# A macaron block (MoE, state-space scan, MoE) on one core: four-column-group tiles with block transposition, a second token buffer and a longer scan

## The reference

```python
def ffn(x):
    scores = sigmoid(x @ w_router.T)
    topk_w, topk_i = top_k(scores, 2)
    topk_w = topk_w / sum(topk_w)
    h = silu(einsum('th,eih->tei', x, wg)) * einsum('th,eih->tei', x, wu)
    out = einsum('te,teh->th', comb, einsum('tei,ehi->teh', h, wd))
    return out + shared_experts(x)

def attn(x):
    p = einsum('bld,ed->ble', x, W_xproj)
    dt, B, C = softplus(p[..., :256]), p[..., 256:272], p[..., 272:]
    h = exp(dt * A) * h + dt * B * x
    y = einsum('bdn,bn->bd', h, C) + D * x

x = x + 0.5 * ffn(layernorm(x))
x = x + attn(layernorm(x))
x = x + 0.5 * ffn(layernorm(x))
```

## Time and profile before

| | |
|---|---|
| time, median of three runs (all three) | 521.38 us (520.27, 521.38, 522.26) |
| span of the profiled execution, first to last instruction | 517.8 us |
| around the span, against the median | 3.6 us |
| PE busy, share of the span | 506.7 us, 98% |
| PE weight loads | 423.2 us, 82% |
| DVE, POOL, ACT busy | 324.0, 231.4, 158.6 us |
| DMA, over the span | 67.91 MB, 131 GB/s |

### The profile page before, as it was taken

The page is one execution under the profiler, slowest core; times in us unless marked ns, Lnnn a source line. Parts: engine busy times, 40 slices in busy tenths (PEclk is TensorE's granted clock), DMA queues, the critical chain, the costliest instruction groups (busy, mean ns, idle before and its releaser), DMA issues.

```text
span 517.8 us, 11713 instructions
## 1 busy us (share of the span) xinstructions
PE 506.7 (98%) x4666; PEld 423.2 (82%) x4667; DVE 324.0 (63%) x658; ACT 158.6 (31%) x337; POOL 231.4 (45%) x208
## 2 busy tenths in 40 slices
PE   8998999999999999999989999999999899999997
PEld 6998996568979999557979799975598899955696
DVE  3844338123747999997679399999967532422225
ACT  1111122221156434553203643445521111122210
POOL 1051000602216999995454289999920650000032
PEclk9999999999999999999999999999999999999999
DMA  7958999512415455541322445545200231210012
GB/s 231 392 231 303 394 389 346 178 59 66 129 36 142 118 139 135 163 117 30 113 63 71 129 94 121 156 131 155 73 22 2 72 101 52 82 42 14 20 54 81
DMA packets 42232, 67.91 MB, mean 131 GB/s; under 512 B 5152, under 2 KB 24992, under 8 KB 42176
## 3 DMA queue, kind: packets, MB, share of 16 engines
q1 hardware_dynamic: 29424, 38.94, 26.5%
q10 hardware_dynamic: 9088, 18.09, 9.4%
q0 software_dynamic: 3664, 10.10, 6.1%
HBM read 48.89 MB, written 18.22 MB: 130 GB/s over the span
## 4 chain that ended last, share of the span: by engine, by line
PE 90%; DVE 6%; DMA 2%; issue 1%; ACT 0%; POOL 0%; DVEq 0%; POOLq 0%; ACTq 0%
PE ps L526 40%; PE ps L551 20%; PE ps L541 14%; PE ps L564 7%; PE ps L570 2%; PE ps L575 2%; PE ps L707 2%; DMA bcb<-bc_rows 1%; PE ps L718 1%; PE ps L748 1%; DVE hb L1054 1%; DMA bc_rows<-hh 1%; DVE hb L1058 0%; PE ps L609 0%; PE ps L759 0%
## 5 line engine op out<-in xcount | busy, mean ns | idle before, releaser
L526 PEld LDWEIGHTS ps<-xt,w_gu 128*128 128x128 f32 x1400 | 161.6, 192 | 5.7 <-issue 3.8
L526 PE MATMUL ps<-xt,w_gu 128*128 128x128 f32 x1400 | 163.8, 276 | 0.4 <-DVE xres L1069 0.4
L1054 DVE SCALAR_TENSOR_TENSOR hb<-hb,ps 128x640 f32<-128x640 f32 x68 | 55.4, 815 | 121.3 <-ACT hb L800 121.2
L551 PE MATMUL ps<-w_dn,hb 128*128 128x256 f32 x520 | 120.8, 380 | 0.0
L551 PEld LDWEIGHTS ps<-w_dn,hb 128*128 128x128 f32 x520 | 94.8, 190 | 10.8
L800 ACT ACTIVATE hb<-ps 128x640 f32<-128x640 f32 x68 | 47.6, 700 | 176.9 <-PE ps L526 163.0
L526 PE MATMUL ps<-xnt,w_gu 128*128 128x128 f32 x680 | 80.5, 276 | 3.0 <-DVE xres L1069 2.7
L1099 DVE TENSOR_TENSOR_SCAN ps<-ps,region 128x512 f32<-128x512 f32 x64 | 78.3, 1223 | 8.1 <-POOL region L1018 6.2
L1032 POOL TENSOR_TENSOR xnt<-xnt,hh 128x512 f32<-128x512 f32 x64 | 82.2, 1286 | 2.5 <-DVE hh L1104 2.5
L526 PEld LDWEIGHTS ps<-xnt,w_gu 128*128 128x128 f32 x680 | 78.7, 192 | 5.5 <-DVE xres L1069 3.1
L998 POOL DMA_INDIRECT region<-yg_rows,ypos x32 | 30.5, 954 | 110.2 <-DMA yg_rows<-ob 88.4
(11 more groups left out here) (112 smaller groups left out, 302.0 us busy)
## 6 DMA issues: line engine op xcount, KB each, us to landing
bcb<-bc_rows SPq DMA_DIRECT2D x22, 512.0 KB, 5.1
region<-bc_rows SPq DMA_DIRECT2D x10, 512.0 KB, 5.0
w_gu<-in_wg ACTq DMA_DIRECT2D x7, 640.0 KB, 9.8
xg<-xg_rows SPq DMA_DIRECT2D x35, 128.0 KB, 4.2
w_gu<-in_wu ACTq DMA_DIRECT2D x7, 640.0 KB, 11.2
w_dn<-in_wd ACTq DMA_DIRECT2D x7, 640.0 KB, 13.8
yg_rows<-ob SPq DMA_DIRECT2D x20, 128.0 KB, 3.5
xg_rows<-bcb SPq DMA_DIRECT2D x1, 2176.0 KB, 14.9
```

The lines of the kernel that those rows point to most:

```text
L526: last = nc.tensor.matmul(gup(p)[:, c * P:(c + 1) * P], w_gu4[:, e, k, c * P:(c + 1) * P], x, start=(k == 0), stop=(k == KC - 1))
L551: ins = nc.tensor.matmul(outp(p), hb[:, p, c * P:(c + 1) * P], w_dn4[:, e, c, :], start=(c == 0), stop=(c == IC - 1))
L1054: nc.vector.scalar_tensor_tensor(out=h, in0=h, scalar=1.0, in1=gup(p)[:, 0:I], op0=ALU.add, op1=ALU.mult).then_inc(s_a, 1)
```

## The change

What it does, part by part:

- Of the four mixed tiles of a segment one stays, `(7, 6, 6)` with the one free group left. The other groups go into three quad tiles of four fixed groups of 32 rows (`QUADS`).
- A quad tile's gate-up takes one group of 32 rows at a time, as the stationary operand of all four column groups; column group q multiplies with the inner columns q x 32 to q x 32 + 31 of each 128 (`quad_piece`), 320 or 160 moving columns in runs of 32. The hidden rows lie in PSUM by quarters; after the products, of which the second is split in two, DVE transposes the 128 x 640 result in blocks of 32 x 32 (`nc.vector.transpose`), and the down-projection `down_quad` reads it as it is.
- `xnt` gets a second buffer, one per half; all shared tiles read it, and the copies to DRAM with their loads, transposes and ACT copies go. The row addresses move by 512 (one `pos` in place of `pos` and `ypos`).
- Gathered rows and the buffers of the overflow loop get the tile `gathered`, and two waits for the result of the scan (`s_yadd`) go. The scratch for POOL's transfer descriptors is set to 4,096 bytes.
- In segment 1 the routed tiles come after two shared ones in place of five. Both scans are dealt out over 13 tiles, and the steps around their ends are set anew.

```diff
-MIXED = [(5, 5, 5), (0, 0, 2), (1, 1, 3), (6, 6, 7)]
+MIXED = [(7, 6, 6)]
+QUADS = [(5, 5, 5, 3), (0, 0, 0, 2), (2, 1, 1, 1)]
...
+QUAD = I // 4
...
-ROUTED = [("whole", e, e) for e in range(WHOLE)] + [("mixed", None, m) for m in range(MT)]
+ROUTED = [("whole", e, e) for e in range(WHOLE)] + [("quad", None, m) for m in range(len(QUADS))] + [("mixed", None, m) for m in range(MT)]
 ORDERS = [SHARED[0] + SHARED[1][:1] + ROUTED + SHARED[1][1:],
-          SHARED[0] + SHARED[1][:1] + ROUTED + SHARED[1][1:],
+          SHARED[0][:2] + ROUTED + SHARED[0][2:] + SHARED[1],
...
-SHARES = [[2, 2, 3, 2, 3, 3, 2, 3, 3, 3, 3, 3], [2, 2, 3, 2, 3, 3, 2, 3, 3, 3, 3, 3]]
+SHARES = [[2, 3, 2, 3, 3, 2, 2, 2, 3, 2, 3, 2, 3], [2, 2, 2, 3, 3, 3, 2, 3, 2, 2, 2, 3, 3]]
...
-    ("X1", 0), ("scan", S1 + 1, S1 + 13, 0), ("first", S1 + 13), ("Y", 0), ("N1", "P", 2), ("N2", "P", 2), ("second", S1 + 13),
-    ("O", 1), ("G", 1), ("first", S1 + 14), ("T", "P", 2), ("second", S1 + 14), ("R1", 2),
-    ("scored and ranked", S1 + 15, 2), ("S", 2, 0), ("second", S1 + 15), ("tiles", S2 - 1, S2),
-    ("C", 1, 0, TT), ("N1", "A", 1), ("S", 2, 1), ("tiles", S2, S2 + 1), ("N2", "A", 1), ("table", 2),
-    ("first", S2 + 1), ("T", "A", 1), ("second", S2 + 1), ("X1", 1),
-    ("scan", S2 + 2, S2 + 14, 1), ("first", S2 + 14), ("Y", 1), ("N1", "P", 3), ("N2", "P", 3), ("second", S2 + 14),
-    ("first", S2 + 15), ("T", "P", 3), ("second", S2 + 15), ("O", 2), ("R1", 3),
+    ("X1", 0), ("scan", S1 + 1, S1 + 14, 0), ("first", S1 + 14), ("Y", 0), ("N1", "P", 2), ("N2", "P", 2),
+    ("second", S1 + 14), ("O", 1), ("G", 1), ("first", S1 + 15), ("T", "P", 2), ("second", S1 + 15), ("R1", 2),
+    ("scored and ranked", S2 - 1, 2), ("second", S2 - 1), ("C", 1, 0, TT), ("N1", "A", 1), ("S", 2, 0), ("N2", "A", 1),
+    ("tiles", S2, S2 + 1), ("table", 2), ("first", S2 + 1), ("T", "A", 1), ("second", S2 + 1), ("X1", 1), ("S", 2, 1),
+    ("scan", S2 + 2, S2 + 15, 1), ("first", S2 + 15), ("Y", 1), ("N1", "P", 3), ("N2", "P", 3), ("second", S2 + 15),
+    ("T", "P", 3), ("O", 2), ("R1", 3), ("scored and ranked", S2 + 16, 3), ("S", 3, 0), ("S", 3, 1), ("second", S2 + 16),
...
-        gat = region[:, 2048:4096].rearrange("p (t s h) -> p t s h", t=TT, s=2)
+        gathered = sb("gathered", [P, TT * 2 * H])
+        gat = gathered[:, :].rearrange("p (t s h) -> p t s h", t=TT, s=2)
...
-        xnt = sb("xnt", [P, KC, HALF])
+        xnt = sb("xnt", [P, 2, KC, HALF])
...
-                        x = xt[:, p, k, :] if loaded(n) else xnt[:, k, t * P:(t + 1) * P]
+                        x = xt[:, p, k, :] if routed(n) else xnt[:, segment(n) % 2, k, t * P:(t + 1) * P]
...
+            def quad_piece(n, j, g0, g1):
+                p, e = n % 2, QUADS[index_of(n)][j]
+                gate = p * 1536 + j // 2 * 512 + j % 2 * QUAD
+                up = p * 1536 + (1024 + j // 2 * QUAD if j % 2 else j // 2 * 512 + 2 * QUAD)
+                for k in range(KC):
+                    w = w_gu4[:, e, k, :].rearrange("p (g c q i) -> p g c q i", g=2, c=IC, q=4)
+                    for q in range(4):
+                        r = q * GROUP
+                        if g1 - g0 == 2:
+                            dst = ps[r:r + GROUP, gate:gate + 4 * QUAD].rearrange("p (g w) -> p g w", g=2)[:, :, 0:QUAD]
+                        else:
+                            a = up if g0 else gate
+                            dst = ps[r:r + GROUP, a:a + QUAD]
+                        last = nc.tensor.matmul(dst, xt[:, p, k, j * GROUP:(j + 1) * GROUP], w[:, g0:g1, :, q, :],
+                                                start=(k == 0), stop=(k == KC - 1))
+                return last
+
+            def gate_up_quad(n, c0):
+                if c0 == 0:
+                    return quad_piece(n, 0, 0, 2)
+                if c0 == 2:
+                    return quad_piece(n, 1, 0, 1)
+                if c0 == 4:
+                    quad_piece(n, 2, 0, 2)
+                    return quad_piece(n, 3, 0, 1)
+                quad_piece(n, 1, 1, 2)
+                return quad_piece(n, 3, 1, 2)
...
+            def down_quad(n):
+                p = n % 2
+                for c in range(IC):
+                    for j in range(4):
+                        r, a = j * GROUP, j * QUAD + c * GROUP
+                        ins = nc.tensor.matmul(outp(p)[r:r + GROUP, :], hb[:, p, a:a + GROUP],
+                                               w_dn4[:, QUADS[index_of(n)][j], c, :],
+                                               start=(c == 0), stop=(c == IC - 1))
+                return ins
...
             def rows_of(n):
-                if n + 2 < TILES and loaded(n + 2):
+                if n + 2 < TILES and routed(n + 2):
...
-                        pool.dma_start(xg_dram[s % 2][0:HALF, :].rearrange("(t p) h -> p t h", p=P),
-                                       xn["P"]).then_inc(s_rows[s], 16)
...
-                nc.vector.tensor_tensor(h, h, gup(p)[:, I:GU], ALU.mult).then_inc(s_h, 1)
+                if kind_of(n) == "quad":
+                    p = n % 2
+                    even, odd = h[:, :, 0:QUAD], h[:, :, QUAD:2 * QUAD]
+                    nc.vector.tensor_tensor(even, even, quad_banks(p)[:, :, 2 * QUAD:3 * QUAD], ALU.mult).then_inc(s_hq, 1)
+                    dve.wait_ge(s_up, n + 1)
+                    nc.vector.tensor_tensor(odd, odd, ps[:, p * 1536 + 1024:p * 1536 + 1024 + 2 * QUAD]
+                                            .rearrange("p (a w) -> p a w", a=2), ALU.mult).then_inc(s_hq, 1)
+                    dve.wait_ge(s_hq, 2 * quads_upto(n))
+                    nc.vector.transpose(hb[:, p, :], hb[:, p, :]).then_inc(s_h, 1)
...
-    nc = bacc.Bacc("TRN2", target_bir_lowering=False, num_devices=1)
+    nc = bacc.Bacc("TRN2", target_bir_lowering=False, num_devices=1, dynamic_dma_scratch_size=4096)
```

More of the change, by code:

```diff
@@ L23 @@
 GROUP = 32
-MIXED = [(5, 5, 5), (0, 0, 2), (1, 1, 3), (6, 6, 7)]
+MIXED = [(7, 6, 6)]
+QUADS = [(5, 5, 5, 3), (0, 0, 0, 2), (2, 1, 1, 1)]
 MT = len(MIXED)
 STATIC0 = WHOLE * P
-FREE0 = STATIC0 + MT * 3 * GROUP
-OWN = [g for tile in MIXED for g in tile]
+QUADS0 = STATIC0 + MT * 3 * GROUP
+FREE0 = QUADS0 + len(QUADS) * P
+OWN = [g for tile in MIXED + QUADS for g in tile]
 ROOM = [(P if e < WHOLE else 0) + GROUP * OWN.count(e) for e in range(E)]
@@ L85, in last_routed, with quads_upto, moves @@
 def last_routed(s):
-    return s * SEG_TILES + max(j for j, t in enumerate(ORDERS[s]) if t[0] == "mixed")
-def loaded(n):
-    return n % SEG_TILES not in DIRECT[segment(n)]
+    return s * SEG_TILES + max(j for j, t in enumerate(ORDERS[s]) if t[0] != "shared")
 def turned(n):
[L95 to L100, removed]
+    return sum(1 for m in range(n + 1) if routed(m))
+def quads_upto(n):
+    return sum(1 for m in range(n + 1) if kind_of(m) == "quad")
 def mixed_upto(n):
     return sum(1 for m in range(n + 1) if kind_of(m) == "mixed")
-def moves(n, q, which):
-    return sum(2 if kind_of(m) == "mixed" else 1 for m in range(n + 1) if m % 2 == q and which(m))
+def moves(n, q):
+    return sum(2 if kind_of(m) == "mixed" else 1 for m in range(n + 1) if m % 2 == q and routed(m))
 def half_states(first, n, part):
@@ L293, in build @@
         s_ones = sem("s_ones")
-        s_rows = [sem(f"s_rows{s}") for s in range(SEGS)]
         s_alog = sem("s_alog")
@@ L402, in load_rows @@
                 else:
-                    a = m * P if kind_of(n) == "shared" else (TT + m) * P
+                    a = QUADS0 + m * P if kind_of(n) == "quad" else m * P
                     sp.dma_start(xg[:, q, :], rows[a:a + P, :]).then_inc(s_xg[q], 16)
@@ L415, in store_rows @@
                 else:
-                    sp.dma_start(rows[m * P:(m + 1) * P, :], ob[:, q, :]).then_inc(s_y[q], 16)
+                    a = QUADS0 + m * P if kind_of(n) == "quad" else m * P
+                    sp.dma_start(rows[a:a + P, :], ob[:, q, :]).then_inc(s_y[q], 16)
             def fetch_rows(m):
-                if m >= TILES or not loaded(m):
+                if m >= TILES or not routed(m):
                     return
                 s = segment(m)
-                if m == first_shared_load(s):
-                    sp.wait_ge(s_rows[s], 16)
                 if m == first_routed(s):
@@ L588, in first_use @@
                             weights_in(e, k)
+                elif kind_of(n) == "quad":
+                    for e in dict.fromkeys(QUADS[index_of(n)]):
+                        weights_in(e, k)
                 elif kind_of(n) == "whole" or index_of(n) == 0:
@@ L659, in second @@
                     rows_of(n)
-                    down_fixed(n).then_inc(s_dn, 1)
+                    down = down_quad if kind_of(n) == "quad" else down_fixed
+                    down(n).then_inc(s_dn, 1)
             def body(n):
@@ L823, in second @@
                     act.wait_ge(s_dn, n + 1)
-                    before = moves(n - 1, q, routed)
+                    before = moves(n - 1, q)
                     if before:
@@ L885, in states @@
```

(4 more changed lines are left out.)

85 lines of the change are left out of this document (41 added, 44 removed).

## The result

The changed kernel takes 527.25 us (median of four runs, 526.70 to 528.22) where the kernel before took 520.83 beside it: the ratio is 1.0088, with a 95% interval of 1.0045 to 1.0132. **It is slower by 0.9%.** The forecast was 521.5; the time lies in the range (513 to 528) and on the number that the second rival gave for two falls of the clock, 527.3.

The account below looks back on a forecast made before the run. It took PE, busy 98% at full clock, as the bound; -9.8 - 1.0 + 0.2 + 4.6 + 5.6 + 0.5 = +0.1 gave 517.9 us of span, 521.5 of time, no difference that can be told; range 513 to 528.

Parts of the forecast that it names:

- the second rival: PE's clock falls to 1.2 GHz in the new idle time, 2.9 us a fall: 524.4 or 527.3 us; chance 0.25.
- Transposes: On PE, 60 of 80 hidden and 30 of 102 row transposes go, 90 x 0.109: -9.8 us.
- width changes: On PE, pairs of changes between 32-column and full-width instructions fall from six to five a segment: -1.0 us.
- quad gate-up: On PE, a quad tile's gate-up takes 4.34 us against 4.31 in a mixed tile: +0.2 us over 12 tiles.
- DVE in a quad tile: Split second product (2 x 0.49) and block transposition (0.82) add 1.0 us a tile on DVE, 88% loaded in scans; nothing booked.
- The price per column: Four side-by-side 32-column matmuls on PE cost 0.84 to 0.93 ns a column; used to price the 320- and 160-column passes.
- End of segment 1: PE waits for an eviction that DVE now does behind the normalization, ahead of the second projection: +4.6 us.
- End of segment 2: A 9.6 us chain from the scan's result to the router's scores has only 3.9 us of PE work beside it: +5.6 us.
- Scatter beside the first B and C rows: Half of segment 2's scatter runs on POOL behind the second projection, sharing DMA engines: 0 to +1.5, +0.5 us taken.
- a slice of the clock below full: Sign that would show the prediction wrong: PE's clock below full in any slice of the profile.
- Narrow matmuls at 57 ns: Rival: 57 ns a matmul is a floor on PE, a quad gate-up takes 5.5 us, 535 in all; chance 0.08.
- the 3.6 us added to the span: The median time lay 3.6 us above the profiled span of 517.8, so the forecast added it to its span.

Follow-up runs that it names:

- fill2: Changed kernel with 10 and 9 matmuls nobody reads put on PE in front of its 4.7 and 4.2 us waits; 524.01 us, ratio 1.0038.
- doses: Kernel before, with DVE held up ahead of three hidden tiles of segment 3 by 11, 17 and 21 unread operations; 533.92 us.
- tail: Changed kernel with segment 2's last down-projection ahead of the transposes of normalized rows and the ranks later, inside a gate-up; 527.83 us, ratio 1.0149.
- s1_12: Changed kernel with the second scan dealt over twelve tiles and the steps behind it as before; 524.92 us, ratio 1.0039.
- both_12: Changed kernel with both scans dealt over twelve tiles and the step order of the kernel before, quad tiles kept; 521.06 us, ratio 0.9978.
- s0_12: Changed kernel with the first scan dealt over twelve tiles and the steps behind it as before; 523.36 us, ratio 1.0030.
- n2_behind: Changed kernel with DVE's next hidden pair and eviction ahead of the normalization at the end of segment 1; 523.04 us, ratio 1.0020.
- best_b: As best_a, but second scan over thirteen tiles, fewer states at its end, its result transposed directly behind it; 516.84 us, ratio 0.9885.
- best_a: Changed kernel with n2_behind's order, one combined segment 1 tile early, and the second scan over twelve tiles in the old order; 517.43 us, ratio 0.9919.

## Why the prediction was right in its range and short in its forecast

- *Transposes, width changes, quad gate-up* (-10.6 together). The quad tile saves 7.51 - 7.02 = 0.49 us, 5.9 in twelve, and thirty row transposes 3.3: -9.2. The difference is the gate-up, 4.47 us in place of 4.34, 1.6 us over twelve tiles. The price per column held within 3%, and the counts held (20 hidden and 72 row transposes).
- *DVE in a quad tile.* The block transposition takes 0.845 us (0.82 taken), a half product 0.49 (0.49). Nothing was booked for it, and over thirteen tiles PE's waits show nothing. The load of 88% held there (86.6 us of work from 148.0 to 245.8 us, the first scan); over twelve tiles PE waits 2.3 us for hidden rows.
- *End of segment 1* (+4.6): 4.72 in the waits. *End of segment 2* (+5.6): 4.15 and 0.69, or 5.3 from start to start less the usual spacing. Both places, both releasers and both sizes held.
- *Scatter beside the first B and C rows* (+0.5). POOL now waits 2.8 us for their landing where it waited 7.7, since it scatters meanwhile; from POOL's store of B and C to the first use it is 8.8 us (290.08 to 298.85), before 8.5, and PE has no wait there: nothing.
- Not foreseen: 0.6 us for the scan's result and an eviction wait of 1.25 us at the end of segment 1.
- **The step that failed is the choice between forecast and rival on the clock.** The forecast let PE stand idle for 4.6 and 5.6 us at full clock, and gave the fall a chance of 0.25. It fell both times, and a slice of the clock below full was one of the prediction's own signs of being wrong. The rival's price, 2.9 a fall, came from the 24 first matmuls; by the rows the first cost 1.7 (eight records +0.71, transposes +0.87, down-projection +0.15) and the second 2.9, and fill2 gives 3.7 for both together in place of the rival's 5.8. The rule that was cited beside it, from the Trainium skill, page TensorE: Matmul & The Clock Gate, section HAM oscillation, says that idle gaps between bursts of matmuls send the clock back to half. This case's rows agree for all the waits of 4.1 to 4.9 us in these profiles. Behind shorter ones they go both ways: nothing behind 1.31 and 2.47 us in doses and 2.00 in tail, a fall behind 2.30 in s1_12 but not in both_12, and a fall in fill2 at the start, where eight matmuls behind a wait of 1.62 us take 2.05.
- *Narrow matmuls at 57 ns.* 96 records in 4.47 us are 46.6 ns each, in a dense run: 57 is no floor. The same page of the Trainium skill, section "Wait — 56ns, not 53.3ns?", has about 62 ns per matmul as a bound in one decode mode. The 46.6 here lie below it, so it does not bind in this kernel.

The ledger: -9.2 of work, +4.7 and +4.8 of waits, +4.6 of clock by the rows, +1.9 of smaller waits make +6.8; the span shows +7.1. That the time met the rival's 527.3 is partly luck. Its span, 523.7, is 1.2 us short of the measured one: it has the saving at 10.6 for 9.2, the clock at 5.8 for 4.6 and none of the smaller waits. And of the 3.6 us added to the span 2.4 are found (527.25 less 524.9).

That the two long waits come from the new ends of the scans is shown by s0_12 and s1_12, which take back the thirteenth tile and the order behind it together. It is the order more than the length: n2_behind and best_b keep thirteen tiles, and the 4.72 us become 1.28, the 4.15 none, with 1.18 ahead of the scan's result and 0.74 ahead of the scores in place of it (best_b also deals out the states otherwise). That the clock falls through idle time is shown by fill2 and doses. Over twelve tiles the quad tiles gain nothing (both_12 beside no_quad). What they gain over thirteen in the order of best_b is not shown, since no run has that order with mixed tiles.

## What to carry to other kernels

On an engine that is busy for 98%, price an idle stretch twice: its length, and what runs slowly behind it. Waits of 1 to 2 us that passed at full clock in one profile don't show the second price, and a profile with a fall in it is a poor source for a sum: s1_12 misled the expectation of best_a by 1.6 us. A saving on the bounding engine that puts work on the next one counts only where that one has time left: here the quad tiles paid 0.5 to 0.6 us each outside the scans, and inside the scans no run shows a gain over before, not even with the order at their ends dealt anew (301.7 us from 17 to 57 in best_b, before 300.9). Before work is moved ahead of a chain, look at what the chain's end is covered by.
